# Two extra TensorE matmuls in every step of a windowed-attention loop, and the score matmul moved to the head of the step

## The reference

```python
# attention on layernorm(x)
g = x @ Wg.T + bg ; v = x @ Wv.T + bv          # split into 16 heads
corr = (g_i . g_j) / (|g_i| |g_j| + 1e-8)      # cosine of every pair
corr = (corr * m + 1) / 2                      # m: j <= i and j >= i - 128
denom = mean_j(corr) + 0.5
fit_i = 1 / (denom_i * sum_i(1 / denom_i))     # a sum over the whole head
attn = softmax(corr * fit_i, masked by m)
x = x + (attn @ v) @ Wo.T + bo
# feed-forward on layernorm(x)
y = square(relu(x @ W_fc.T)) @ W_proj.T        # 1024 -> 4096 -> 1024
# five steps of a spiking neuron on y, count / 5, added to x
```

## Time and profile before

| | us |
|---|---|
| median of 2 runs | 1704.08 (1701.37 and 1706.8) |
| the profiled execution's own time | 1703.45 |
| its span, slowest core (core 1) | 1701.3 |
| spans of all eight cores | 1686.0 to 1701.3 |
| attention stage, first L478 to first output-projection work | about 418 to 906 |

### The profile page before, as it was taken

One profiled execution on the slowest core, in us unless ns is written; L12 is line 12 of the kernel. 1 busy time (PEld: TensorE's weight loads), 2 busy tenths in 40 slices (PEclk: granted clock), 3 DMA queues, 4 the chain that ended last, 5 costly groups with the idle time before them and its releaser, 6 DMA issues.

```text
span 1701.3 us, 16533 instructions; the slowest of 8 cores (1686.0 to 1701.3 us)
## 1 busy us (share of the span) xinstructions
PE 1025.9 (60%) x4632; PEld 433.9 (26%) x4632; DVE 680.8 (40%) x1639; ACT 673.5 (40%) x1467; POOL 131.5 (8%) x216
## 2 busy tenths in 40 slices
PE   0024655593555555555556787888688768878800
PEld 0012222241222222222222333333233323333300
DVE  1301121201555555555543002079405960395098
ACT  1354333231566666666665543054303540342000
POOL 1011221111000000000000000111011101101100
PEclk9999778796555555555557898999899989999955
DMA  9887665444000000000003334444544434445301
GB/s 188 215 172 150 99 99 111 111 100 98 1 1 1 1 1 1 1 1 1 1 1 116 108 118 141 125 136 136 173 124 128 154 140 148 124 149 173 111 24 50
DMA packets 78908, 158.69 MB, mean 93 GB/s; under 512 B 38627, under 2 KB 38884, under 8 KB 78820
## 3 DMA queue, kind: packets, MB, share of 16 engines
q0 software_dynamic: 63824, 106.97, 26.2%
q1 hardware_dynamic: 14996, 50.68, 9.0%
HBM read 147.15 MB, written 33.55 MB: 106 GB/s over the span
## 4 chain that ended last, share of the span: by engine, by line
DMA 29%; PE 23%; DVE 21%; issue 12%; ACT 8%; another core or an unknown queue 4%; POOL 1%; DVEq 1%; ACTq 0%; SPq 0%; POOLq 0%
PE psY L834 8%; DMA wpb<-wprojC 7%; DMA wstg<-wfcT 6%; DMA wstg<-wprojT 5%; PE psY L796 5%; ACT PT L585 4%; DMA wfcb<-wfcC 4%; DVE memb L873 3%; PE psPV L599 3%; DVE t1b L870 3%; DMA wfcC<-wstg 3%; DMA wprojC<-wstg 3%; DVE accb L881 3%; PE psPT L577 2%
## 5 line engine op out<-in xcount | busy, mean ns | idle before, releaser
L796 PE MATMUL psY<-x2nT,wfcb 128*128 128x512 bf16 x1024 | 238.5, 391 | 52.1 <-DMA wfcb<-wfcC 51.1
L834 PE MATMUL psY<-wpb,h_sb 128*128 128x512 bf16 x1024 | 237.2, 388 | 37.9 <-DMA wpb<-wprojC 37.0
L599 PE MATMUL psPV<-PT,v_sb 128*64 128x128 bf16 x512 | 104.5, 308 | 97.7 <-ACT PT L585 97.7
L484 DVE SCALAR_TENSOR_TENSOR C<-psD,maskA_sb 128x256 f32<-128x256 f32 x240 | 100.9, 421 | 153.0 <-PE psD L478 150.0
L526 ACT ACTIVATE ebf<-C,fit 128x256 f32<-128x256 f32 x256 | 151.5, 592 | 2.3 <-DVE em L565 0.6
L796 PEld LDWEIGHTS psY<-x2nT,wfcb 128*128 128x128 bf16 x1024 | 99.6, 100 | 190.2 <-issue 86.1
L577 PE MATMUL psPT<-ident_sb,em 128*128 128x128 bf16 x512 | 98.2, 295 | 81.5 <-DVE em L565 81.5
L834 PEld LDWEIGHTS psY<-wpb,h_sb 128*128 128x128 bf16 x1024 | 98.6, 100 | 175.2 <-issue 72.6
L805 ACT ACTIVATE frb<-psY 128x512 f32<-128x512 f32 x128 | 76.6, 599 | 118.6 <-PE psY L796 118.5
L852 ACT ACTIVATE y<-psY 128x512 f32<-128x512 f32 x32 | 16.1, 624 | 265.3 <-PE psY L834 265.3
L862 DVE TENSOR_SCALAR spkA<-y 128x1024 f32<-128x1024 f32 x16 | 11.1, 694 | 274.9 <-ACT y L852 273.6
(11 more groups left out here) (99 smaller groups left out, 1213.8 us busy)
## 6 DMA issues: line engine op xcount, KB each, us to landing
wfcb<-wfcC POOLq DMA_DIRECT2D x64, 512.0 KB, 4.2
wpb<-wprojC POOLq DMA_DIRECT2D x64, 512.0 KB, 4.1
xa<-xin SPq DMA_DIRECT2D x32, 512.0 KB, 4.7
wstg<-wfcT POOLq DMA_DIRECT2D x32, 256.0 KB, 5.2
xpair<-xin SPq DMA_DIRECT2D x8, 1024.0 KB, 12.4
wfcC<-wstg POOLq DMA_DIRECT2D x16, 512.0 KB, 3.2
wstg<-wprojT POOLq DMA_DIRECT2D x16, 512.0 KB, 5.3
wprojC<-wstg POOLq DMA_DIRECT2D x16, 512.0 KB, 2.9
```

Source lines behind the costliest of these rows:

```text
L484: msk=(mask0_sb if qt == 0 else maskA_sb): h.scalar_tensor_tensor(C_sb[hb][:, 256 * qt:256 * qt + 256], psD[qb][:], 1.0, msk[:], ALU.mult, ...
L599: mpv = b.op("T", lambda h, h_i=h_i, hp=hp, qt=qt, q4=q4, pb=pb, half=half: h.matmul(psPV[pb][hp:hp + 64, 128 * (q4 % 2):128 * (q4 % 2) + ...
L796: mmt = b.op("T", lambda h, f=f, fp=fp, k=k, gi=gi: h.matmul(psY[f % 2][:], wfcb[fp % 2][:, 1024 * (f % 2) + 128 * k:1024 * (f % 2) + 128 ...
L834: last = b.op("T", lambda h, f=f, f2=f2, tti=tti, nh=nh, pj=pj: h.matmul(psY[pj][:], h_sb[:, 512 * f + 128 * tti:512 * f + 128 * tti + 128 ...
```

## The change

Three edits. A PSUM tile `psH` (128x512) is added. In the loop `emit_pass1` is called ahead of `emit_pv`. At the end of each of the 256 steps two matmuls 128x512 are added that multiply the identity by a slice of `woT_sb` into `psH`; nobody reads `psH`. The waits of such a matmul are the one added before it (on TensorE's own semaphore), the load of `woT_sb`, and `c_last[i % 2]`, DVE's last write to `C` in heads of that parity. In the changed kernel lines behind the first edit are one higher (L478 becomes L479).

```diff
@@ build_core
     psPV = [psb_("psPV0", (128, 256)), psb_("psPV1", (128, 256))]
     psS = psb_("psS", (128, 512))
+    psH = psb_("psH", (128, 512))
...
+    tok_heat = [None]
     for i in range(NSTEP + 23):
+        if i < NSTEP:
+            emit_pass1(*hq(i))
         if i >= 22 and i - 22 < NSTEP:
             emit_pv(*hq(i - 22))
-        if i < NSTEP:
-            emit_pass1(*hq(i))
         if i >= 17 and i - 17 < NSTEP:
             emit_e(*hq(i - 17))
...
         if i < NSTEP and hq(i)[1] == NT - 1:
             emit_stats(hq(i)[0])
+        if i < NSTEP:
+            for _ in range(2):
+                tok_heat[0] = b.op("T", lambda h: h.matmul(
+                    psH[:], ident_sb[:], woT_sb[:, 0:512],
+                    start=True, stop=True),
+                    waits=[tok_heat[0], tok_wo, c_last[i % 2]])
```

## The result

The changed kernel takes 1863.6 us (median of 11 runs, 1854.8 to 1877.3) against 1705.2 for the kernel before: the ratio is 1.094, 95% interval 1.091 to 1.098. The forecast was 1868. The sum came out within 5 us, but two of its terms were wrong, and they had opposite signs: the reordering was worth more than nothing, and the wait for `c_last` cost something. Some executions of every kernel are longer, with a lower granted clock on the cores of one die; the ratios leave them out and the medians do not, which matters for the last experiment alone, where half of the runs are such.

The account below looks back on a forecast made before the run. The attention stage was taken as bound by a ring of waits, PE at 1.2 GHz. Fifteen heads 141, first steps 22.4 and last steps 1.3 gave 165 us on 1703.5: 1868; own range 1826 to 1895, widened to 1742 to 1895.

Parts of the forecast that it names:

- The ring: Attention stage: no engine is full, a ring of waits sets the two-step period, 3.41 us before, 4.61 after.
- pv(E) to pv(O): PE, from the even step's two L599 matmuls to the odd step's: 0.98 us before, 2.18 after.
- ring one: PE's stretch pv(E) to pv(O), then ACT's L608, L526, L585 (2.43 us) to the next even L599: 3.41 us.
- h1 to h2: From the first to the second added matmul of a step, which waits for the first: 0.77 us.
- The clock: TensorE in the attention stage: stays at 1.2 GHz, the main choice, chance 0.72.
- Rival A: Attention stage: the clock goes to 2.4 GHz, period 3.71 us, total 1744, up to 1757; chance 0.16.
- The reordering alone is worth 0: L478 ahead of L599 in the loop: at best 1 or 2 us over the stage, since ring one keeps 3.41.
- ring two: L478, DVE's C, L550, em, odd step's L577, L585, even step's L599, back to L478: also 3.41 us.
- pt(O): The odd step's two L577 matmuls on PE, fed by em; forecast to have about 1 us to spare.
- The added wait: First added matmul's wait for c_last in the loop: cost 0, upper bound 0.2 us in every period.
- Statistics and first steps: Statistics at each head's end: 2.2 us a head; first sixteen steps, without L599 and L577: +22.4 us.
- The last steps' 1.3: Last 23 steps: only step 255's two added matmuls stand ahead, +1.3 us.

Follow-up runs that it names:

- e3: Changed kernel with the two added matmuls only in even steps: 1822.8 us, ratio 1.073 to the kernel before.
- e4: Changed kernel with the two added matmuls only in odd steps: 1712.7 us, ratio 1.012 to the kernel before.
- e6: Changed kernel without each added matmul's wait for the one before it: 1780.5 us, ratio 1.044 to the kernel before.
- e8: Changed kernel with four added matmuls, in odd steps only, waiting only for the load of woT: 1732.7 us, ratio 1.016 to the kernel before.
- e10: e9 with four added matmuls in odd steps in place of six, statistics still filled: 1716.5 us, ratio 1.006 to the kernel before.
- e7: Changed kernel with four added matmuls in every step, waiting only for the load of woT: 1762.2 us, ratio 1.032 to the kernel before.
- e5: Changed kernel without the added matmuls' wait for c_last: 1850.0 us, ratio 1.084 to the kernel before.
- e2: Kernel before with the added matmuls and all their waits, but emit_pv still ahead of emit_pass1: 1906.2 us, ratio 1.120.
- e1: Kernel before with the reordering only, no added matmuls: 1678.8 us, ratio 0.987.
- e12: e9 with three of an odd step's six added matmuls moved ahead of pt(O): 1655.1 us over six runs, ratio 0.965 to the kernel before.
- e9: Changed order; unchained added matmuls, six per odd step, none in even ones, more in statistics and before the stage: 1692.6 us, ratio 0.992.

## Why the prediction was right, and where it was not

**The ring.** Right as a mechanism. pv(E) to pv(O) was to go from 0.98 to 2.18 and the rest to stay 2.43; in long heads the trace has 2.13 and 2.47, period 4.60 against 4.61. e3 and e4 show that the pair on that stretch carries the cost: without the odd pair the periods are 4.61 and 4.33. That 2.43 came so near 2.47 is luck, for it was read in a short head, where ring one's own rest is 2.2.

**h1 to h2.** Right: 0.77 taken, 0.76 to the weights and about 0.79 to the matmul measured.

**The clock.** Right that it stays at 1.2 GHz: 0.50 on all eight cores. The reason given was the pause behind each h1. e6 takes the wait away, and the pause with it, and the clock moves, so the wait is shown to be what kept it low. That the pause itself does it is not shown: e6's work is also denser, and e8 and e10, without any pause between their four, had stretches of 40 us and more at 0.50 on some cores. Rival A's reason, that PE hardly rests any more, did not raise it at a busy share of 88%. Rival A's period of 3.71 was not tested as such; e7, at 3.57 and 3.84, has two more matmuls on the stretch but no pause. Digit 5 of the page begins in the eleventh slice, and not in the tenth as the prediction reads it; nothing hangs on that.

**"The reordering alone is worth 0".** Wrong; it is worth 22 us. The step that failed is the length of ring one: "(2.43 us)" for L608, L526 and L585 held a wait for pt(O), which is ring two's. Ring one without it is 3.17 in every second head. Two rings of 3.41 stood in one row, and I took them for two equal bounds when the one was measured through the other. The end of a head, where the reordering brings the statistics forward by 0.56, was not looked at.

**The added wait, "I take 0".** Wrong by some 10 us, with the same root: the slack was worked out for an ACT part of 2.43, and in the heads where it is 2.2 the next pv(E) is earlier and the hold of h1 comes through (2.18 + 0.18 against 2.2 is the 0.16 of e5). Its upper bound, 0.2 a period, covered it. What it costs without the reordering stands in e2's expectation and not in the prediction: periods of 5.1 and 4.87, measured 5.13 and 4.85.

**Why the sum held all the same.** Partly by luck. In the changed kernel the ACT part is 2.2 in every second head, which takes 0.28 off the period (4.33 in e5 against 4.61), and the C wait gives 0.16 of it back. The net is 4.49 in these heads instead of 4.61, 7 or 8 us over eight of them, which is the 6 us by which the fifteen heads were over-forecast. Against e1, with its 1678.8, the added matmuls cost 185 us, some 20 more than the 165 of the forecast, and the reordering gives 22 that the forecast does not have. The two cancel because the new period was built from its links, 2.18 and 2.43, and not as the old one and a price.

**Statistics and first steps.** 2.2 us a head for the statistics; measured 38.7 less eight periods of 4.55 is 2.3. First steps 22.4 against 21.9. The last steps' 1.3 was 0: from the last statistics instruction to the last copy both kernels take 33.8, so the two matmuls behind L508 lie beside ACT's own work.

## What to carry to other kernels

In a stage in which no engine is full, price added work by the ring that it stands on, not by the engine's total: against the same order without them, the same pair of matmuls cost 144 us on one side of a wait and 34 on the other. Compare with a kernel that differs in the one thing alone: against the kernel before, the 34 looked like 12. If work is added for the clock's sake, issue it back to back, as e6, e7 and e12 do, without waits on its own engine, in the place where the engine waits, and split it around the instruction that others wait for. Where two rings show the same length, ask of each wait in the row which of the two set it; one of them may be shorter than it looks.

## What the runs showed of the hardware that was not expected

- At PE busy 88% (507.7 of 580.2 us) the granted clock was 0.50 from end to end; in e6 at 45.5 of 60 us busy it was 0.84. In the kernels with the chain (the changed one, e2, e3, e4, e5), with a pause of some 0.35 us behind the first matmul of each pair, it stayed at 0.50 on all cores. In e6 and e8, back to back, it rose and fell again; six in each odd step with filled statistics (e9, e12) had 1.00 on every core from 500 us on.
- ACT's distances depend on the head: in e1, L609 to L527 to L586 are 0.50 and 0.71 in one kind of head and 0.38 and 0.58 in the other. The heads of one kind use the other `C` buffer and the other half of the partitions; which of these is behind it was not tried and stays open.
- Matmuls that nobody reads can pay: e12 issues 986 of them (its trace's count on one core) and is 24 us faster than the same order with none (35 by the runs that the ratios go by).
